# Second message-passing loop: 16 counted runs and 10 gathered tiles a pair, node rows as three bf16 parts

## The reference, cut to what matters

```
h = x_tangent @ W.T + b                            # x_tangent: the layer norm, relu and logmap0 of the nodes
deg = segment_sum(ones, dst) + segment_sum(ones, src);  dinv = max(deg, 1) ** -0.5
msg = h[src] * (dinv[src] * dinv[dst])[:, None]
out = segment_sum(msg, dst)
norm = ||out||;   x = x + tanh(norm) / max(norm, 1e-15) * out
```

## Time and profile before

| | us |
|---|---|
| three runs, median (lowest to highest) | 882.84 (882.05 to 884.15) |
| the profiled execution, its own time | 881.85 |
| its span | 880.0 |
| PE busy | 793.6 (90%) |
| DVE busy | 698.5 (79%) |
| ACT busy | 532.8 (61%) |
| POOL busy | 580.6 (66%) |

### The profile page before, as it was taken

How to read it: one execution, slowest core, us unless ns; L and a number is a source line. 1 busy time by engine, 2 the same in 40 slices (tenths; PEclk the granted TensorE clock), 3 DMA queues, 4 the chain that set the end, 5 groups by cost and what they waited for, 6 DMA issues and landing times.

```text
span 880.0 us, 21604 instructions
## 1 busy us (share of the span) xinstructions
PE 793.6 (90%) x5339; PEld 607.0 (69%) x5339; DVE 698.5 (79%) x2575; ACT 532.8 (61%) x1360; POOL 580.6 (66%) x597
## 2 busy tenths in 40 slices
PE   5659988999999999999999999997399999999995
PEld 2236766777767777777776776775268788888875
DVE  8835777778778778767877877878989989898984
ACT  4386656666666666666666666643856656565641
POOL 0176777777777777777777777750077777777772
PEclk9857999999999999999999999998789999999999
DMA  6652455644644544444454454432222222222221
GB/s 176 207 154 85 121 126 121 138 122 120 131 129 120 137 125 119 123 133 120 114 137 125 117 135 127 118 106 79 76 59 67 74 66 75 63 75 63 75 63 45
DMA packets 103597, 96.01 MB, mean 109 GB/s; under 512 B 35964, under 2 KB 87393, under 8 KB 103553
## 3 DMA queue, kind: packets, MB, share of 16 engines
q0 software_dynamic: 25600, 66.10, 27.4%
q1 hardware_dynamic: 77961, 29.51, 13.5%
HBM read 84.40 MB, written 11.15 MB: 109 GB/s over the span
## 4 chain that ended last, share of the span: by engine, by line
PE 78%; DVE 9%; ACT 5%; issue 3%; DMA 3%; SPq 1%; POOL 0%; POOLq 0%; DVEq 0%; ACTq 0%
PE ps_r L1870 11%; PE ps_q L1850 10%; PE ps_s L1827 10%; PE ps_r L2030 10%; PE ps_f L1905 6%; PE ps_f L2043 4%; PE ps_q L2013 4%; PE ps_s L1837 4%; PE ps_c L1819 4%; PE ps_s L2013 3%; ACT ST L1620 3%; PE ps_b L2013 2%; PE ps_f L1929 1%; PE ps_f L1928 1%; PE ps_c L1815 1%
## 5 line engine op out<-in xcount | busy, mean ns | idle before, releaser
L815 POOL DMA_INDIRECT kv<-kv_tab,idx x416 | 409.8, 985 | 176.4 <-issue 111.9
L863 POOL DMA_INDIRECT kv<-hs_tab,idx x176 | 170.5, 969 | 108.5 <-DMA hs_tab<-qkv 52.3
L1620 ACT ACTIVATE ST<-ps_s,imj 128x512 f32<-128x512 f32 (+1 forms) x128 | 77.1, 602 | 128.0 <-PE ps_s L1837 126.3
L1850 PE MATMUL ps_q<-qwin,ST 128*128 128x128 f32 x832 | 128.6, 295 | 8.1 <-DMA qwin<-q_tab 4.0
L1850 PEld LDWEIGHTS ps_q<-qwin,ST 128*128 128x128 f32 x832 | 105.4, 196 | 25.2 <-issue 24.8
L1603 ACT ACTIVATE S<-iota,nloc 128x128 f32<-128x128 f32 x384 | 122.0, 389 | 0.0
L1870 PE MATMUL ps_r<-wv,S 128*128 128x137 f32 x832 | 112.7, 289 | 0.0
L1870 PEld LDWEIGHTS ps_r<-wv,S 128*128 128x128 f32 x832 | 105.0, 195 | 8.0 <-issue 7.0
L1827 PE MATMUL ps_s<-rep_hi,iota_b 128*128 128x512 bf16 x410 | 110.2, 387 | 0.0
L1092 DVE TENSOR_TENSOR prod<-kv,ps_q 128x512 f32<-128x512 f32 (+1 forms) x128 | 71.5, 575 | 31.6 <-PE ps_q L1850 29.4
L2030 PE MATMUL ps_r<-qkv,xt 128*128 128x128 f32 x800 | 92.0, 276 | 0.8 <-ACT xt L1745 0.8
(11 more groups left out here) (278 smaller groups left out, 1339.5 us busy)
## 6 DMA issues: line engine op xcount, KB each, us to landing
kv<-kv_tab,idx POOLq DMA_INDIRECT x416, 2.8
attr_s<-in_attr SPq DMA_DIRECT2D x32, 192.0 KB
kv<-hs_tab,idx POOLq DMA_INDIRECT x176
kv_tab<-qkv SPq DMA_DIRECT2D x4, 640.0 KB, 3.4
x_tab<-x SPq DMA_DIRECT2D x32, 64.5 KB
qwin<-q_tab SPq DMA_DIRECT2D x32, 64.0 KB
xwin<-in_x SPq DMA_DIRECT2D x32, 64.0 KB
xwin<-x_tab SPq DMA_DIRECT2D x32, 64.0 KB
```

What stands on the lines that cost most here:

```text
L815: pool.indirect_dma_start(out=kv[:, b, t, :], out_offset=None, in_=kv_tab, in_offset=bass.IndirectOffsetOnAxis(ap=idx[:, b, t:t + 1], axis ...
L863: pool.indirect_dma_start(out=kv[:, j, t, 0:D], out_offset=None, in_=hs_tab, in_offset=bass.IndirectOffsetOnAxis(ap=idx[:, j, t:t + 1], ax ...
L1620: A.activation(ST[:, b, t0:t1, :], row_index(c), ACT.Abs, bias=imj[:, 0:1], scale=-1.0).then_inc(s_sta, 1)
L1850: mm = M.matmul(ps_q[c % 2][:, (t - t0) * D:(t - t0 + 1) * D], ST[:, b, t, :], qwin[:, b, :], start=True, stop=True)
```

## The change

**Runs.** `T1` goes from 15 to 16 and `T2` from 11 to 10: one more tile of the odd group is counted, one fewer gathered. The places of the rows are no longer 32 wide everywhere but given in a table, from 14 rows wide (first run) to 34 (the last three). The element order of a key changes from (block, row) to (row, block), so that a piece of the key one-hot for one bank is contiguous, and so is the bank. The seven banks now hold 14, 17, 20, 20, 20, 20 and 17 rows, 128 in all, so that nothing of `counts` has to be blanked.

**Three parts.** `hs_t` is split into three bf16 parts, whose sum is the float32 value (`hs3`): ACT rounds to the first part, DVE subtracts it, ACT rounds the rest to the second part, DVE subtracts again and writes the third, each in five pieces of 128x640. `counts` becomes float16 (small whole numbers). `counted_sums` then multiplies blocks of `counts` by 384 columns of bf16, 25 matmuls into `parts` (three sums side by side in one bank), and window 2n adds the three by a TENSOR_REDUCE in the place of the copy.

**Squares on ACT.** `zz` and the square on DVE go. ACT computes the square of R times dinv[dst] with its row sum (`square`), one for each window: the first at the head of its pair, before the seven copies, the second after the one-hots of gathered tiles 0 to 3. DVE's chain waits for both (`s_ss1`). dinv[dst] is then multiplied into the factor by one more operation on 128x2 numbers, and the output is made from `R`.

**Around it.** A third tile's edges are loaded to `src_more` and `dst_more` in the first loop (two more transfers of 8 KB by SP, in turns 12 and 13). `xn` and `hT` share a tensor with `counts`, `line` one with `hs3`, and `dloc_rows` one with `y_out`. 13 more memsets of 128x1 stand at DVE's start. Two of the waits between POOL's gathers name other banks (`BANK_DONE`).

```diff
-N1 = 17
+N1 = 14
-W = 32
-T1 = T + 2
+T1 = T + 3
+WAYS = 3
-BANK_DONE = {7: 2, 8: 3, 9: 5, 10: 6}
-ROW0 = [min(max(round((t + 0.5) * P * N / E - W / 2), 0), P - W) for t in range(T1)]
+BANK_DONE = {7: 2, 8: 4, 9: 6}
+ROWS_OF = [(0, 14), (4, 22), (9, 31), (16, 38), (22, 46), (30, 56), (37, 63), (43, 71), (51, 79), (58, 88), (65, 95),
+           (72, 104), (79, 111), (86, 120)] + [(94, 128)] * (MORE - 1)
+BANK_EDGES = [0, 14, 31, 51, 71, 91, 111, P]
...
-        counts = xt[:, :, 0:D]
+        counts = xh[:].rearrange("p a e -> p (a e)").bitcast(F16)[:, 0:NT * P].rearrange("p (n e) -> p n e", n=NT)
+        left = xt[:, :, 0:D]
...
-                V.tensor_scalar(oh_key(t), iota_key, run_col(src_key, n, t), None, ALU.is_equal).then_inc(s_ohr, 1)
+                V.tensor_scalar(oh_key(t), iota_key[:, 0:NT * WIDE[t]], run_col(src_key, n, t), None, ALU.is_equal).then_inc(s_ohr, 1)
...
+            def without_first(c):
+                dve.wait_ge(s_hi, c + 1)
+                V.tensor_tensor(left[:, chunk(c), :], hs_t[:, chunk(c), :], hs3[:, chunk(c), 0, :], ALU.subtract).then_inc(s_left, 1)
+            def third_part(c):
+                dve.wait_ge(s_mid, c + 1)
+                V.tensor_tensor(hs3[:, chunk(c), 2, :], left[:, chunk(c), :], hs3[:, chunk(c), 1, :], ALU.subtract).then_inc(s_hs3, 1)
-            def window(g, b, i, st, more):
+            def window(g, b, more):
                 dve.wait_ge(s_agg1, g + 1)
-                V.tensor_copy(R[:, b, 0:D], sums[b]).then_inc(s_R1, 1)
-                dve.wait_ge(s_R1, g + 2)
-                dve.wait_ge(s_xw1[i], 32 * ((g - i) // 4 + 1) if known(g) else (g + (4 - i)) * 8)
-                st.then(V.tensor_scalar(zz[:, b, :], R[:, b, 0:D], xwin[:, i, D:D + 1], None, ALU.mult))
+                if not (known(g) and g < 2):
+                    dve.wait_ge(s_y1, g - 1)
+                if b == 0:
+                    V.tensor_reduce(R[:, b, 0:D], parts.rearrange("p (k d) -> p d k", k=WAYS), AX_X, ALU.add).then_inc(s_R1, 1)
+                else:
+                    V.tensor_copy(R[:, b, 0:D], sums[b]).then_inc(s_R1, 1)
                 if more:
                     shift1(g + 2, b)
-                st.mark(V.scalar_tensor_tensor(out=hsq[:, b, :], in0=zz[:, b, :], scalar=1.0, in1=zz[:, b, :], op0=ALU.mult,
-                                               op1=ALU.mult, accum_out=ss2[:, b:b + 1]))
...
-                st.sync()
+                dve.wait_ge(s_ss1, 2 * n + 2)
...
+                st.then(V.tensor_tensor(a_, a_, xwin[:, 2 * j:2 * j + 2, D], ALU.mult))
...
             with dve.If_eq(in_order, 1):
-                for n in range(2):
-                    for t in range(T1):
-                        run_one_hots(n, t)
+                for c in range(NT // PCH):
+                    without_first(c)
+                for t in range(T1):
+                    run_one_hots(0, t)
+                for c in range(NT // PCH):
+                    third_part(c)
                 shift1(0, 0)
                 shift1(1, 1)
+                for t in range(T1):
+                    run_one_hots(1, t)
...
+            def square(g, b, i):
+                act.wait_ge(s_R1, g + 2)
+                act.wait_ge(s_xw1[i], rows_in(g, i))
+                A.activation(hsq[:, b, :], R[:, b, 0:D], ACT.Square, scale=xwin[:, i, D:D + 1], accum_out=ss2[:, b:b + 1])\
+                    .then_inc(s_ss1, 1)
...
                 def pair(n, j, more=True, far=True):
+                    square(2 * n, 0, 2 * j)
                     if more:
                         count_copies(n + 1, range(CB))
                     if far:
-                        one_hots1(n + 2, j, CH2[:2])
+                        one_hots1(n + 2, j, CH2[:1])
+                    square(2 * n + 1, 1, 2 * j + 1)
+                    if far:
+                        one_hots1(n + 2, j, CH2[1:2])
                     norm_part(n)
...
-                    mm = M.matmul(sums[0], counts[:, i, :], hs_t[:, i, :], start=(i == 0), stop=False)
+                    mm = M.matmul(parts, counts[:, i, :], hs3[:, i, :, :].rearrange("p k d -> p (k d)"), start=(i == 0), stop=False)
```

More of the change, by code:

```diff
@@ L117 @@
 FINISHED = [k for now in COUNT_ORDER for k, t in now if t == LAST[k]]
-assert FINISHED == list(range(CB))
+assert FINISHED == list(range(CB)) and max(hi - lo for lo, hi in BANK_ROWS) * NT <= 512
+assert WIDE[T:] == [WMAX] * MORE and ROW0[T + 1:] == [ROW0[T + 1]] * (MORE - 1)
 FREED = [1 + max(k for k in range(CB) if t in TOUCH[k]) for t in range(T1)]
+FIRST_KEYS = max(t for t in range(T1) if sum(WIDE[:t]) * NT <= 2 * T * P * 2)
 ROUND = 12582912.0
@@ L309, in build @@
         src_key = runs(place(late, 1))
-        iota_key = place(late, 2, NT * W // 2).bitcast(F16)
+        iota_key = place(late, 2, NT * WMAX // 2).bitcast(F16)
         sm2 = sb("sm2", [P, 4, 2])
@@ L471, in build @@
         s_cnt = sem("s_cnt")
-        s_cblank = sem("s_cblank")
+        s_hi = sem("s_hi")
+        s_left = sem("s_left")
+        s_mid = sem("s_mid")
+        s_hs3 = sem("s_hs3")
         s_cntc = sem("s_cntc")
@@ L513, in build @@
         qkv_banks = [ps_q[0], ps_q[1], ps_r, ps_c]
-        sums = [ps_r[:, 0:D], ps_f[:, D:2 * D]]
+        parts = ps_r[:, 0:WAYS * D]
+        sums = [ps_r[:, 0:D], ps_f[:, 3 * D:4 * D]]
         count_banks = [ps_f, ps_q[0], ps_q[1], ps_s[0], ps_s[1], ps_b, ps_c]
@@ L682, in _ @@
                 turn(11, 1)
-                assert MORE == 2
-                with sp.Fori(6, GROUPS // 2 - 1) as n:
+                load_more(src_more, late_src, 2)
+                turn(12, 0)
+                load_more(dst_more, late_dst, 2)
+                turn(13, 1)
+                assert MORE == 3
+                with sp.Fori(7, GROUPS // 2 - 1) as n:
                     turn(2 * n, 0)
@@ L1483, in _ @@
             V.memset(R[:, 1, :], 0.0).then_inc(s_R1, 1)
-            for k in range(0, NT * W, P):
-                w = min(P, NT * W - k)
+            for k in range(0, NT * WMAX, P):
+                w = min(P, NT * WMAX - k)
                 M_.mark(V.tensor_scalar(iota_key[:, k:k + w], iota[:, 0:w], float(k), None, ALU.add))
@@ L1526, in pair @@
                     set_rest(n + 2, j)
-                window(2 * n + 1, 1, 2 * j + 1, st, more)
+                window(2 * n + 1, 1, more)
                 v_, y_, t_, a_ = [sm2[:, i, :] for i in range(4)]
-                st.sync()
+                dve.wait_ge(s_ss1, 2 * n + 2)
                 st.then(V.tensor_scalar(v_, ss2[:], 1e-30, None, ALU.max))
@@ L1747, in _ @@
             with act.If_eq(in_order, 1):
+                for c in range(NT // PCH):
+                    first_part(c)
                 one_hots1(0, 0)
+                for c in range(NT // PCH):
+                    second_part(c)
+                count_copies(0, range(CB))
                 one_hots1(1, 1)
-                count_copies(0, range(CB))
                 def pair(n, j, more=True, far=True):
+                    square(2 * n, 0, 2 * j)
                     if more:
```

76 lines of the change are left out of this document (47 added, 29 removed).

## The result

The changed kernel takes 878.31 us (median; the kernel before, timed beside it on the same chip, 884.68). The ratio is 0.9938, with a 95% interval of 0.9915 to 0.9961: 5.5 us less, between 3.5 and 7.5. The medians differ by 6.4, because they are over all 20 executions of each kernel and the ratio leaves out those more than 1.5% above the fastest. The forecast was 7.0 less, 875.8 us. The profiled execution took 878.26 us, with a span of 876.4 (before: 881.85 and 880.0).

What follows compares the result with a forecast made beforehand. PE, POOL and DVE were taken as co-bound at 14.0 to 14.4 us a pair, DVE longest afterwards at 13.65. Ahead +6.4, loop -11.6, end -1.9, small items +0.1: -7.0, so 875.8 us; 865 to 884 holds 8 in 10.

Steps and rivals of the forecast that it cites:

- (a): DVE's one-hots in a pair: 16 runs with 10850 elements take 7.90 us against 7.93 before, no change.
- (b): DVE at window 2n: reduction over 384 PSUM elements, then shift, 0.66 us in all (0.5 to 0.9), gain 0.59.
- (c): DVE at window 2n+1, copy to chain: waits for ACT's square, 0.95 us (0.8 to 1.3) against 1.27, gain 0.32.
- (d): One more step in DVE's chain of 128x2 operations: 0.20 us a pair lost.
- PE and POOL: Their own time in a pair after the change: PE 12.2 us, POOL 12.7 (ten gathers of 1.27), idle 0.9.
- Ahead of the loop: DVE before window 0: ten subtractions of 640 elements cost 7.5 us, window 0 comes at 660.3, 6.4 lost.
- The end: From window 0 of pair 14 to the end: 21.5 us instead of 23.4, 1.9 won.
- A: Rival: DVE isn't the bound, it falls to POOL's 12.7 us a pair; 13.3 more won, 862 us; chance 0.08.
- B: Rival: key one-hots on DVE lose their rate at new widths, 2.1 us more a pair, 910 us; chance 0.07.
- C: Rival: PE's clock falls because of its gaps, some 23 us a pair, time near 1000 us; chance 0.02.
- D: Rival: readout 0.6, reduction 0.9, subtractions 8.5 give the gain back; 14.1 to 14.3 a pair, 883 to 886 us; chance 0.15.
- The 13.9: The pair's period in us if multiply and square stayed on DVE by the skill's rule, instead of 13.65.

Runs made afterwards that it cites:

- more_dve: The changed kernel with two more one-hots of 850 elements a pair on VectorE: 14.38 us a pair, ratio 1.002 to the kernel before.
- less_dve: The changed kernel with two Newton steps instead of three in the second loop's inverse square root: 13.09 us a pair, ratio 0.9843 to the kernel before.
- squares_act: The kernel before with only the squares moved to ScalarE and the factor step added on VectorE: 14.23 us a pair, ratio 0.9963.
- parts_alone: The changed kernel with 15 counted runs, 11 gathered tiles and squares back on VectorE: 14.08 us a pair, ratio 1.004 to the kernel before.
- squares_dve: The changed kernel with the squares put back on VectorE and the factor step gone: 14.75 us a pair, ratio 1.0169 to the kernel before.

## Why the prediction was right

**The bound.** Three co-bound engines before, VectorE after: shown from both sides by more_dve and less_dve, and by squares_act, where some 0.9 us less on VectorE moved the pair by 0.25 only, and parts_alone, where PE's relief moved it by 0.40 only.

**Parts of VectorE's pair.** (a) One-hots 7.90 forecast, 7.96 measured. (b) Reduction and shift 0.66 and 0.66; the reduction takes 0.55 us where I interpolated 0.54. (c) Copy to chain 0.95 forecast, 0.83 measured: the square takes 0.40 and its readout 0.19, which I had only bounded (0.1 to 0.6). (d) The new step costs 0.37 from start to start, not 0.20. Two more semaphore waits (`s_xw1`) stand between it and its predecessor; they are the likely reason, since in squares_dve, where they stand ahead of the output rows, these too come 0.37 behind the factor (0.31 before the change). The two misses cancel, 0.12 one way and 0.17 the other, so the exactness of 13.65 and 13.64 is luck; the terms were right to 0.2.

**PE and POOL.** `counted_sums` 4.24 (forecast 4.2), ten gathered tiles 2.47 (2.4), PE's busy time 12.1 a pair (12.2). POOL waits at the first gather of a pair for 0.6 to 1.5 us where its usual pause is 0.30, and for the indices, as forecast (0.9). Its steps without the waits were 1.29 us, not 1.27, so ten of them are 12.9, not 12.7; it stood 0.7 us below VectorE.

**Ahead of the loop.** From the first VectorE instruction that needs the node rows to window 0 it takes 663.81 - 640.15 = 23.66; before, 653.94 - 637.03 = 16.91. Cost 6.75 against 6.4; the ten subtractions are 7.60 against 7.5. The other 3.1 us by which window 0 is late were there at 640, ahead of all the work of the second loop.

**The end.** 21.66 against 21.5, with two waits for the gathered sums, 3.48 and 3.47; before they were 2.77 and 3.42, the second of them in the earlier trace rows.

**Sum.** In the trace: 9.87 lost up to window 0, 11.77 won in 14 pairs, 1.70 won at the end, together -3.6 and -6.7 without the 3.1. The ratio says -5.5 (3.5 to 7.5).

**The rivals.** A fell (VectorE is the bound). B fell: no width lost its rate, 0.31 ns an element at 350 to 850. By the condition of the Trainium skill ("Vector Engine (DVE) Microarchitecture Reference", section 5.1), even widths keep it. The trace agrees, with 494 ns for 850. C fell in the changed kernel (1.00 from 660 to 868 us), but squares_dve had 0.91 in half of its stretches, and the five runs in which PE idled 2.74 to 6.54 us before the last tiles paid 1.5 to 2.3 us there. D fell, all its three prices came out below it. The Trainium skill's rule for ScalarE ("ScalarE: Activation LUTs", "Rules for kernel authors") is to use VectorE for `mul`. The trace agrees for one operation (0.40 + 0.19 us on ScalarE, 0.28 + 0.08 on VectorE in squares_dve) and not for the pair: with the squares on VectorE it is 14.5 to 14.75, which squares_dve measured. The 13.9 that the prediction gave for this was a wrong sum: it takes back the gain at window 2n+1 but not most of the 0.59 at window 2n, which comes from the same two operations. By its own terms it is 13.65 + 0.59 + 0.32 - 0.20 = 14.36, and some 0.3 more for the reduction in the place of the copy.

## What to carry to other kernels

Read the period of every engine, not its busy share: an engine at 90% whose small operations wait for each other can be the bound, and the cheapest gain is then to issue independent work between the dependent steps (here 8 us of 212, with no instruction removed). When several engines lie within a few per cent, a change pays in full only if it relieves all of them, and each part alone can measure as next to nothing. A gatherer with a head start hides its lag for many rounds; look for it at the end of the loop, and price the idle time that it gives PE there.
